# Loading rows of a fused attention and mixture-of-experts kernel by tiles, and adding the experts' rows ahead of the shared part

## The chip, the core and the metric

The kernel runs on one core of a Trainium2 chip. The metric is the time on the device from launch to end, in microseconds, as the median of several runs. The core's engines are TensorE (PE in the profile; PEld is its weight load), VectorE (DVE), ScalarE (ACT), GpSimd (POOL) and SyncE (SP), which here only issues DMAs. PEq, ACTq, POOLq and SPq in a row mean the engine's own instruction queue.

## The reference

```python
# x: 8 x 512 x 512, float32; T = 4096 tokens in all
x = x + layernorm(attention(layernorm(x, g_in), attn_bias, mask) @ Wo, g_out)   # gives "x1"
logits = (x @ wt.T + repeat(g @ wg.T)) / 2                 # 8 experts
topk_w, topk_idx = top_k(softmax(logits), 2); topk_w /= topk_w.sum()
y = sum over the 2 chosen experts e of
      topk_w * ((leaky(x @ w_gate[e]) * (x @ w_up[e])) @ w_down[e])
p = (leaky(x @ sw_gate) * (x @ sw_up)) @ sw_down           # shared part, every token
out = x + y + p
```

The attention has 16 heads of 64 with one key and one value head. An expert is 256 wide, the shared part 512.

## The kernel before

The work is done in stages, one after the other, each a block that all engines leave and enter together: projections, attention, output, route, experts, shared. Every product of importance is made three times (high half by high half, high by low, low by high), with operands split by ACT (the rounded high half) and DVE (the low half, by subtraction). The unit of work is a tile of 128 tokens; there are 32, four to a sequence ("batch", index b).

- **Output stage** (`stage_output`). Per tile t: ACT and DVE split `o_in`, the attention's result; PE multiplies it with Wo (L1251 to L1253, 24 products); DVE takes statistics (L1172) and normalizes (L1182); POOL multiplies by g and adds x (L1152, L1155), which gives x1; PE transposes x1 (L1270), ACT copies the transposed tile (L1220), PE makes the logits (L1276). SP's queue is written out by hand, in this order for a step: load o_in of tile t + 2, store x1 of t - 1, load x of t + 1, store x1T of t - 2. After tiles 0 to 15 and again after tiles 16 to 19 SP waits for the stores of the first eight tiles and issues two loads of 1 MB, x1T and x1 of batch 0 and of batch 1 (L141, L136), for the next stage.
- **Route stage** (`stage_route`). DVE finds each token's two experts and its places in the lists of the experts, in a long chain of small operations. In parallel the shared part of batches 0 and 1 is computed: ACT and DVE split x1T in four chunks of 128 columns (L1416, L1569), PE makes gate and up products (L1619 to L1621), then the down products, and ACT and POOL put the result plus x1 into `partial`. PE also counts (L1660, after `both_ready`) and finds the tokens of each tile of the experts (L1667). `leak` and `hidden` are separate buffers.
- **Expert stage** (`stage_experts`). 71 tiles of 128 gathered rows. POOL gathers the rows of a tile by an indirect DMA (L149), two buffers; PE transposes them (L1873), makes gate and up, then down products for the tile before. The weights of three experts fit. SP issues the loads of experts 1 and 2 (four DMAs of 1.5 MB) and only then reports expert 0 as ready (`make_ready`, L1764). ACT copies a finished tile and stores it in `ys_d`; at the end it waits for all these stores.
- **Shared stage** (`stage_shared`). Six steps u; step u computes the shared part of batch u + 2. `gate`/`up` products for four column blocks j (24 products each), then down products for four tiles. Meanwhile the two expert rows of each token are gathered from `ys_d` (POOL, two indirect DMAs a tile, two sets of buffers) and added by DVE, weighted (L2066, two operations a tile): for the early batches to `partial` between the gate blocks, in steps 0 and 1; for batch u + 2 to `total`, after DVE has added the PSUM result and x1 (L2096). A tile can be stored only then, and the x1 of batch b + 2 is loaded behind the four stores.

What starts the next batch's split is one semaphore for both loads:

```python
act.wait_ge(x1_loaded[k], 32 * ((u + EARLY_B) // 2 + 1))
```

Of the kernel before, what the change touches and what calls it, by code (L numbers as in the profile page):

```python
# [29 lines left out]
P = 128  # L30
# [26 lines left out]
EARLY_B = 2  # L57


def build(nc, x, fside, cond, mask, g_in, null_bias, Wq, Wkv, Wo, g_out,  # L60
# [16 lines left out]
    with ExitStack() as ctx:  # L77
# [39 lines left out]
        partial = ctx.enter_context(nc.sbuf_tensor("partial", [P, EARLY_B * TB, D], F32))  # L117
        with ExitStack() as held:
# [12 lines left out]
                          rows, xg, rows_ready, xg_loaded, partial, x_added)  # L131
        stage_shared(nc, dram, psum, ident, spare, shared, route, x1, x1_loaded, x1T, partial, out)
# [860 lines left out]
def stage_output(nc, x, cond, wo_stage, wo_loaded, g_out, wt, wg, sw_gate, sw_up, sw_down, shared, dram, psum, ident,  # L993
                 pow_half, eps, spare, logits, x1_in, x1_loaded, x1T_in):

    with ExitStack() as ctx:
# [3 lines left out]
        def sem(name):  # L1000
# [25 lines left out]
        ln_stats, ln_moments, ln_shifted, ln_rstd = (sem("ln3_stats"), sem("ln3_moments"), sem("ln3_shifted"),  # L1026
                                                     sem("ln3_rstd"))
        y_ready, y_scaled, x1_ready = sem("y_ready"), sem("y_scaled"), sem("x1_ready")
# [8 lines left out]
        EARLY = T // 4  # L1037
# [29 lines left out]
        def _(sp):  # L1067
# [7 lines left out]
            def store_x1(t, k):  # L1075
                sp.wait_ge(x1_ready, t + 1)
                sp.dma_start(dram["x1"][bass.ds(t * P, P), :], x1[k][:]).then_inc(x1_stored[k], 16)
# [21 lines left out]

            def load_shared(n, w):  # L1100
                sp.dma_start(w_stage[n % 2][:], w.rearrange("(c p) n -> p c n", p=P)).then_inc(shared_loaded[n], 16)
# [32 lines left out]
        def _(pool):  # L1134
# [9 lines left out]
            def step(t, k, m):  # L1144
                pool.wait_ge(ln_moments, t + 1)
                pool.tensor_tensor(out=rstd[:, k:k + 1], in0=moments[:, k, 1:2], in1=eps[:, 0:1], op=ALU.add
                                   ).then_inc(ln_shifted, 1)
                pool.wait_ge(ln_shifted, t + 1)
                pool.tensor_tensor(out=rstd[:, k:k + 1], in0=rstd[:, k:k + 1], in1=pow_half[:, 0:1], op=ALU.pow
                                   ).then_inc(ln_rstd, 1)  # L1150
                pool.wait_ge(y_ready, t + 1)
                pool.tensor_tensor(out=x1[k][:], in0=x1[k][:], in1=g_rows[:], op=ALU.mult).then_inc(y_scaled, 1)  # L1152
                pool.wait_ge(y_scaled, t + 1)
                pool.wait_ge(x_loaded[k], 16 * m + 16)
                pool.tensor_tensor(out=x1[k][:], in0=x1[k][:], in1=x_in[k][:], op=ALU.add).then_inc(x1_ready, 1)  # L1155
# [4 lines left out]
        def _(dve):  # L1160
# [7 lines left out]
            def step(t, k, m):  # L1168
# [9 lines left out]
                dve.wait_ge(ln_rstd, t + 1)  # L1178
# [62 lines left out]
        def _(pe):  # L1241
# [23 lines left out]
            def transpose_x1(t, k):  # L1265
                pe.wait_ge(x1_ready, t + 1)
# [32 lines left out]
def stage_route(nc, dram, psum, ident, logits, shared, route, experts, experts_loaded, x1, x1_loaded, x1T,  # L1299
# [4 lines left out]
    with ExitStack() as ctx:  # L1304
# [53 lines left out]
        hidden = [sb(f"hidden4_{i}", [P, S]) for i in range(2)]  # L1358
# [19 lines left out]
        def _(pool):  # L1378
# [23 lines left out]
            pool.wait_ge(x1_loaded[0], 32)  # L1402
# [10 lines left out]
        def _(act):  # L1413
            def split_x_high(b, c):
                act.wait_ge(x1_loaded[b], 32)
# [201 lines left out]
        def _(pe):  # L1617
# [5 lines left out]
            def gate_up(b, j):  # L1623
# [47 lines left out]
            pe.wait_ge(xT_lo_ready, DC)  # L1671
# [6 lines left out]
            pe.wait_ge(xT_lo_ready, 2 * DC)  # L1678
# [11 lines left out]
def stage_experts(nc, dram, psum, ident, spare, experts, experts_loaded, route, x1, x1_loaded, x1T, rows,  # L1690
                  xg, rows_ready, xg_loaded, partial, x_added):
# [3 lines left out]
    with ExitStack() as ctx:  # L1695
# [12 lines left out]
        y_out = [sb(f"y_out{i}", [P, D]) for i in range(2)]  # L1708
# [7 lines left out]
        ys_stored = [sem(f"ys_stored{i}") for i in range(2)]  # L1716
# [43 lines left out]
        def _(sp):  # L1760
# [406 lines left out]
```

## Time and profile before

| | |
|---|---|
| median of 3 runs | 1713.74 us (1711.5 to 1713.85) |
| the profiled execution, its own time | 1716.19 us |
| its span, first to last instruction | 1714.5 us |
| mean granted TensorE clock | 0.97 |
| PE busy | 1592.4 us, 93% |
| DVE, POOL, ACT busy | 57%, 44%, 42% |

All times inside the execution are microseconds from the start of the span. The output stage begins about 780, the route stage at 1040, the expert stage at 1123, the shared stage at 1492. A row of the timeline gives start, duration, engine, line and operation, output and inputs; the brackets at its end say how long the engine had been idle and what ended that. Consecutive equal instructions are merged in one row (x4).

### The profile page before, as it was taken

To read this page: it belongs to the slowest core of one execution; us is meant where nothing else is said; L and a number is where in the kernel's file an instruction comes from. 1 tells how busy PE (TensorE), PEld (TensorE's weight loads), DVE (VectorE), ACT (ScalarE), POOL (GpSimd) and SP (SyncE) were. 2 spreads that over 40 slices of the span, in tenths; PEclk is the share of its full clock that TensorE was granted. 3 is DMA by queue.
4 is the path that set the end of the run, shared out by engine and by line. 5 is a ranking of instruction groups with operands and counts; after the bars stand their busy time and mean duration, and the time that the engine had idled before them with its cause. 6 is when DMAs were issued, how large, how long until landed. Compare 5 with 4: busy or idle time off the path is not lost. (4 is left out here: it accounts for less than half of the span.)

```text
span 1714.5 us, 36472 instructions
## 1 busy us (share of the span) xinstructions
PE 1592.4 (93%) x10236; PEld 1336.2 (78%) x10237; DVE 973.7 (57%) x2954; ACT 712.9 (42%) x1823; POOL 747.9 (44%) x1305
## 2 busy tenths in 40 slices
PE   6899996999999999996999997989999999899997
PEld 4778876998898898895887786867777788687776
DVE  5544525877777777775654456823333334365664
ACT  2232325776777777773222222123333433311211
POOL 1000245786686686784554461432222222234222
PEclk9999998999999999998999998999999999999999
DMA  6676668787676677776556652053475533247433
GB/s 228 208 240 214 217 218 225 220 234 198 204 228 199 207 225 203 213 222 173 194 185 212 214 168 105 0 221 104 177 278 211 208 109 102 98 159 228 151 109 113
DMA packets 181195, 318.11 MB, mean 186 GB/s; under 512 B 17298, under 2 KB 64962, under 8 KB 179028
## 3 DMA queue, kind: packets, MB, share of 16 engines
q1 hardware_dynamic: 150754, 251.59, 45.9%
q0 software_dynamic: 11200, 35.73, 7.0%
q10 hardware_dynamic: 19122, 29.52, 5.0%
q8 instruction: 36, 0.59, 0.1%
q14 instruction: 83, 0.68, 0.1%
HBM read 195.38 MB, written 121.39 MB: 185 GB/s over the span
## 5 line engine op out<-in xcount | busy, mean ns | idle before, releaser
L811 DVE CUSTOM_DVE_ANT_0 scores<-psum,resident 128x514 f32<-128x514 f32 (+3 forms) x512 | 245.8, 489 | 96.3 <-issue 95.9
L885 ACT ACTIVATE probs<-scores,lowest 128x514 f32<-128x514 f32 (+3 forms) x512 | 282.9, 555 | 28.4 <-DVE lowest L811 23.3
L783 POOL TENSOR_SCALAR probs<-probs,rsums 128x512 f32<-128x512 f32 (+3 forms) x512 | 263.0, 524 | 0.0
L932 PE MATMUL psum<-keys,queries 128*128 (+4 forms) x640 | 220.7, 353 | 26.7 <-DMA queries_and_ones<-q_hi_d 17.4
L944 PE MATMUL psum<-ident,probs 128*128 128x128 f32 x1280 | 234.3, 282 | 1.6 <-POOL probs L783 1.3
L932 PE MATMUL psum<-keys_lo_and_mask,queries_and_ones 128*128 (+4 forms) x640 | 184.9, 297 | 0.0
L944 PEld LDWEIGHTS psum<-ident,probs 128*128 128x128 f32 x1280 | 151.5, 142 | 28.4 <-POOL probs L783 20.2
L964 PE MATMUL psum<-probsT,v_now 128*64 128x128 f32 x2560 | 168.3, 278 | 0.9 <-DVE probsT L826 0.9
L932 PEld LDWEIGHTS psum<-keys,queries 128*128 128x128 f32 x640 | 127.2, 199 | 33.9 <-issue 18.4
L964 PEld LDWEIGHTS psum<-probsT,v_now 128*64 128x64 f32 x2560 | 137.5, 137 | 14.5 <-issue 1.9
L894 ACT ACTIVATE probsT<-psum 128x512 f32<-128x512 f32 (+2 forms) x192 | 93.8, 489 | 115.4 <-PE psum L944 102.9
L1878 PE MATMUL psum<-expert_weights,xT_hi 128*128 x284 | 122.1, 430 | 5.6 <-SPq L1764 4.5
L932 PEld LDWEIGHTS psum<-keys_lo_and_mask,queries_and_ones 128*128 128x128 f32 x640 | 125.4, 196 | 0.0
L826 DVE COPY probsT<-psum 128x512 f32<-128x512 f32 (+1 forms) x192 | 121.6, 633 | 2.7 <-PE psum L944 2.6
L1838 DVE TENSOR_TENSOR hT_lo<-psum,hT_hi 128x256 fp32r<-128x256 f32 x71 | 30.1, 424 | 161.0 <-ACT hT_hi L1795 161.0
L1251 PE MATMUL psum<-wo_hi,oT_hi 128*128 128x512 f32 x256 | 108.7, 425 | 13.6 <-DVE oT_lo L1164 13.6
L1880 PE MATMUL psum<-expert_weights,xT_lo 128*128 x284 | 112.8, 397 | 0.0
L1879 PE MATMUL psum<-expert_weights,xT_hi 128*128 x284 | 112.4, 396 | 0.0
L146 POOL COPY slot_rows<-slot_tokens 128x1 int32 (+1 forms) x71 | 13.0, 183 | 227.9 <-PE psum L1873 226.2
L376 DVE SCALAR_TENSOR_TENSOR q_lo<-psum,q_hi 128x512 fp32r<-128x512 f32 x64 | 43.9, 687 | 113.1 <-ACT q_hi L482 113.0
L556 PE MATMUL psum<-xT_hi,wq_hi 128*128 128x512 f32 x256 | 105.3, 411 | 1.6 <-DVE xT_lo L368 1.6
L482 ACT ACTIVATE q_hi<-psum 128x512 fp32r<-128x512 f32 x64 | 38.3, 598 | 160.7 <-DMA q_lo_d<-q_lo 84.2
(242 smaller groups left out, 3705.8 us busy)
## 6 DMA issues: line engine op xcount, KB each, us to landing
ys_d<-y_out ACTq DMA_DIRECT2D x71, 256.0 KB
q_hi_d<-q_hi SPq DMA_DIRECT2D x64, 256.0 KB, 2.4
q_lo_d<-q_lo SPq DMA_DIRECT2D x64, 256.0 KB, 2.8
queries<-q_hi_d SPq DMA_DIRECT2D x64, 256.0 KB, 3.7
queries<-q_lo_d SPq DMA_DIRECT2D x64, 256.0 KB, 4.2
queries_and_ones<-q_hi_d SPq DMA_DIRECT2D x64, 256.0 KB, 4.5
oT_d<-o_out SPq DMA_DIRECT2D x64, 256.0 KB, 2.3
o_in<-oT_d SPq DMA_DIRECT2D x32, 512.0 KB, 4.8
```

What stands on the lines that cost most here:

```text
L556: pe.matmul(out, hi[:, c, :], xT_hi[k][:, c, :], start=(c == 0), stop=False)
L783: pool.tensor_scalar(out=row, in0=row, scalar1=rsums[:, n % RING:n % RING + 1], scalar2=1.0, op0=ALU.mult, op1=ALU.mult).then_inc(probs_sc ...
L811: dve.tensor_tensor_reduce(out=scores[n % 4][:, 0:CK[i]], in0=score_psum(n), in1=bias_of(resident, i, h), scale=1.0, scalar=3.0e38, op0=AL ...
L826: dve.tensor_copy(dst, src).then_inc(probsT_odd, 1)
L885: act.activation(probs[n % RING][:, 0:CK[i]], scores[n % 4][:, 0:CK[i]], ACT.Exp, bias=lowest[:, n % 4:n % 4 + 1], scale=-1.0, accum_out=s ...
L932: last = pe.matmul(whole[:, lo:hi], qs[hp % 2][:, n % 2, i * P:(i + 1) * P], ks[:, bass.ds((b % 2) * (AHEAD + S) + lo, hi - lo)], start=(p ...
L944: last = pe.transpose(probsT_bank[g % NB][:, at + j * P:at + (j + 1) * P], probs[n % RING][:, AHEAD + j * P:AHEAD + (j + 1) * P], ident[:])
L964: last = pe.matmul(o_bank[head * DH:(head + 1) * DH, cols], v_now[:, j * DH:(j + 1) * DH], probsT[half][:, at:at + P], start=(j == 0), sto ...
L1251: pe.matmul(out_bank[k], oT_hi[k][:, c, :], wo_hi[:, c, :], start=(c == 0), stop=False)
L1878: pe.matmul(out, hi, experts[:, bass.ds(at, D)], start=start, stop=False)
L1879: pe.matmul(out, hi, experts[:, bass.ds(at + EW, D)], start=False, stop=False)
L1880: return pe.matmul(out, lo, experts[:, bass.ds(at, D)], start=False, stop=stop)
```

## The change

Four places are changed.

1. Output stage: instead of two loads of 1 MB at two points, each step of tiles 12 to 27 ends with one load of 256 KB: x1T of one tile after an even step, x1 of one tile after an odd one; eight for each batch (`EARLY_LOADED` is the count that their readers wait for). The waits for the stores of tiles 0 to 7 are gone. Several semaphores of POOL and DVE are merged into one that counts both steps.
2. PE waits for each chunk of the split x in turn, in the first gate products, instead of for all four (route and shared stage). In the route stage `hidden` is put on `leak`'s place.
3. Expert stage: SP reports expert 0 first, then waits until the gathers of tiles 0 and 2 have landed, and only then loads experts 1 and 2. ACT no longer waits for its last stores; POOL waits for them at the start of the shared stage.
4. Shared stage: four sets of gather buffers instead of two. For batch u + 2 DVE first makes x1 plus the two expert rows, between the gate blocks, into a `total` of four tiles; the PSUM result is added last. The early batches' adds come after it, tile by tile. The load of the next x1 waits for the adds to x1 and goes ahead of the stores.

```diff
-        EARLY = T // 4
+        EARLY = 6
...
+            def load_x1T_tile(b, j):
+                sp.dma_start(x1T_in[b][:, bass.ds(j, 1), :, :].bitcast(F32).rearrange("p a c n -> p (a c n)"),
+                             dram["x1T"][bass.ds(j + TB * b, 1)].rearrange("a p n -> p (a n)")).then_inc(x1_loaded[b], 16)
...
-            for b in range(EARLY_B):
-                with sp.Fori((2, EARLY)[b], (EARLY, EARLY + 2)[b]) as m:
-                    for k in range(2):
-                        step(2 * m + k, k, m)
-                for i in range(2):
-                    sp.wait_ge(x1_stored[i], 16 * EARLY_B * TB // 2)
-                    sp.wait_ge(x1T_stored[i], 16 * EARLY_B * TB // 2)
-                sp.wait_ge(wo_lo_ready, len(WO_PARTS))
-                load_x1T(sp, dram, x1T_in, b, b, x1_loaded)
-                load_x1(sp, dram, x1_in, b, b, x1_loaded)
-            with sp.Fori(EARLY + 2, T // 2 - 1) as m:
+            with sp.Fori(2, EARLY) as m:
                 for k in range(2):
                     step(2 * m + k, k, m)
-            for t in range(T - 2, T):
+            sp.wait_ge(wo_lo_ready, len(WO_PARTS))
+            for b in range(EARLY_B):
+                with sp.Fori(0, TB) as j:
+                    step(2 * j + 2 * (EARLY + TB * b), 0, j + EARLY + TB * b)
+                    load_x1T_tile(b, j)
+                    step(2 * j + 2 * (EARLY + TB * b) + 1, 1, j + EARLY + TB * b)
+                    load_x1_tile(b, j)
+            for t in range(2 * (EARLY + TB * EARLY_B), T):
                 step(t, t % 2, t // 2)
...
-        hidden = [sb(f"hidden4_{i}", [P, S]) for i in range(2)]
+        hidden = leak
...
                     for c in range(DC):
+                        if j == 0 and dst is gate_bank:
+                            pe.wait_ge(xT_lo_ready, DC * b + c + 1)
...
-            pe.wait_ge(xT_lo_ready, DC)
...
+            make_ready(0)
+            sp.wait_ge(xg_loaded[0], 32)
             for e in range(1, PLACES):
                 load_expert(sp, dram, experts, e, experts_loaded)
-            make_ready(0)
             make_ready(1)
...
-            for k in range(2):
-                act.wait_ge(ys_stored[k], 16 * ((N + 1 - k) // 2))
...
+        RING = 4
-        TILES = [TB * b + t for u in range(LAST + 1) for b in ([u] if u < EARLY_B else []) + [u + EARLY_B]
+        TILES = [TB * b + t for u in range(LAST + 1) for b in [u + EARLY_B] + ([u] if u < EARLY_B else [])
                  for t in range(TB)]
...
             def step(u, k, m):
+                b = u + EARLY_B
                 if u + 2 <= LAST:
                     sp.wait_ge(xT_lo_ready, DC * u + DC)
-                    load_x1T(sp, dram, x1T, u + EARLY_B + 2, k, x1_loaded)
-                if u < EARLY_B:
-                    for t in range(TB):
-                        store(u, t, partial[:, TB * u + t, :])
-                b = u + EARLY_B
+                    load_x1T(sp, dram, x1T, b + 2, k, x1_loaded)
+                    sp.wait_ge(first_added, place(TB * b + TB - 1) + 1)
+                    load_x1(sp, dram, x1, b + 2, k, x1_loaded)
                 for t in range(TB):
-                    store(b, t, total[t % 2])
-                if u + 2 <= LAST:
-                    load_x1(sp, dram, x1, b + 2, k, x1_loaded)
+                    sp.wait_ge(total_ready, TB * u + t + 1)
+                    store(b, t, total[k][:, t, :], k)
+                    if u < EARLY_B:
+                        sp.wait_ge(picked_added, place(TB * u + t) + 1)
+                        store(u, t, partial[:, TB * u + t, :], k)
...
+            for k in range(2):
+                pool.wait_ge(ys_stored[k], 16 * ((USED_TILES + 1 - k) // 2))
             for q in TILES:
                 gather(q)
...
-                    if u < EARLY_B:
-                        add_picked(partial[:, TB * u + j, :], TB * u + j)
+                    if j == 0:
+                        dve.wait_ge(x1_loaded[k], x1_there(u))
+                        if u >= 2:
+                            dve.wait_ge(out_stored[k], 16 * STORES[u])
+                    add_experts(total[k][:, j, :], x1[k][:, j, :], TB * (u + EARLY_B) + j)
                 for t in range(TB):
...
-                    dve.tensor_tensor(out=total[n], in0=y_bank[n], in1=x1[k][:, t, :], op=ALU.add).then_inc(y_added, 1)
-                    dve.wait_ge(y_added, done)
-                    add_picked(total[n], q)
+                    dve.wait_ge(y_full, TB * u + t + 1)
+                    dve.wait_ge(picked_added, place(TB * (u + EARLY_B) + t) + 1)
+                    dve.tensor_tensor(out=total[k][:, t, :], in0=y_bank[t % 2], in1=total[k][:, t, :], op=ALU.add
+                                      ).then_inc(total_ready, 1)
+                    if u < EARLY_B:
+                        add_experts(partial[:, TB * u + t, :], partial[:, TB * u + t, :], TB * u + t)
```

`add_experts(acc, before, q)` waits for both gathers of tile q, then makes acc = weight 0 x row 0 + before and acc = weight 1 x row 1 + acc.

## Rows read from the trace of the kernel before

**Rows 1.** The page's first part: busy time of each engine.

```profile
PE 1592.4 (93%) x10236; PEld 1336.2 (78%) x10237; DVE 973.7 (57%) x2954; ACT 712.9 (42%) x1823; POOL 747.9 (44%) x1305
```

**Rows 2.** Busy per engine in a window: PEclk, DMA share, GB/s last.

```profile
1130.00:1140.00 10.00, 7.08 (x27) 5.49 (x27) 2.79 (x6) 1.76 (x4) 3.88 (x5) 0.83 1.02 429
```

**Rows 3.** Timeline, output stage, DVE: start, duration, instruction, [idle before <-releaser].

```profile
913.58 0.70 DVE L1172 BATCH_NORM_STATS2 stats<-psum 128x6 f32<-128x512 f32 x1 [1.85 <-PE psum L1253]
...
927.03 0.70 DVE L1172 BATCH_NORM_STATS2 stats<-psum 128x6 f32<-128x512 f32 x1 [5.78 <-PE psum L1253]
...
940.82 0.70 DVE L1172 BATCH_NORM_STATS2 stats<-psum 128x6 f32<-128x512 f32 x1 [1.67 <-PE psum L1253]
...
947.68 0.70 DVE L1172 BATCH_NORM_STATS2 stats<-psum 128x6 f32<-128x512 f32 x1 [1.85 <-PE psum L1253]
```

**Rows 4.** Timeline, output stage, SP's queue and ACT.

```profile
909.64 0.35 SPq L1069 DMA_DIRECT2D o_in<-oT_d  x1
...
919.30 1.15 ACT L1213 ACTIVATE oT_hi<-o_in 128x512 fp32r<-128x512 f32 x2 [10.08 <-DMA o_in<-oT_d]
...
935.12 0.34 SPq L1069 DMA_DIRECT2D o_in<-oT_d  x1
```

**Rows 5.** DMA issues, 850 to 906 us: last column us to landing.

```profile
o_in<-oT_d SPq DMA_DIRECT2D x8, 512.0 KB, 4.6
...
x1T_d<-x1T SPq DMA_DIRECT2D x8, 256.0 KB, 3.0
```

**Rows 6.** Timeline, end of the output stage and start of the route stage.

```profile
1039.57 0.42 DVE L1201 TENSOR_TENSOR logits<-psum,group_logits 128x256 f32<-128x256 f32 x1
...
1040.30 2.19 ACT L1416 ACTIVATE expert_weights<-x1T_in 128x512 fp32r<-128x512 f32 x4 [3.01 <-PEq L996]
...
1040.96 2.50 DVE L1569 TENSOR_TENSOR x1T_in<-x1T_in,expert_weights 128x512 fp32r<-128x512 f32 x4 [0.96 <-ACT expert_weights L1416]
...
1043.51 0.80 PE L1619 MATMUL psum<-expert_weights,shared_hi 128*128 128x512 f32 x1 [4.30 <-DVE x1T_in L1569]
```

**Rows 7.** Timeline, start of the expert stage: a gather, then PE's transposes of x rows.

```profile
1124.90 1.00 POOL L149 DMA_INDIRECT xg<-x_d,slot_rows  x1 [0.15 <-issue]
...
1127.53 0.60 PE L1873 MATMUL psum<-ident,xg 128*128 128x128 f32 x4
...
1134.56 0.66 PE L1873 MATMUL psum<-ident,xg 128*128 128x128 f32 x4 [2.92 <-DMA xg<-x_d,slot_rows]
...
1141.02 0.60 PE L1873 MATMUL psum<-ident,xg 128*128 128x128 f32 x4
...
1145.88 0.60 PE L1873 MATMUL psum<-ident,xg 128*128 128x128 f32 x4
```

**Rows 8.** Timeline, end of the expert stage and start of the shared stage.

```profile
1490.22 0.35 ACTq L1810 DMA_DIRECT2D ys_d<-y_out  x1
1492.72 0.63 ACT L2034 ACTIVATE xT_hi<-x1T_in 128x512 fp32r<-128x512 f32 x1 [2.53 <-PEq L1695]
...
1496.00 0.80 PE L2106 MATMUL psum<-xT_hi,shared_hi 128*128 128x512 f32 x1 [6.44 <-DVE xT_lo L2059]
```

**Rows 9.** Timeline of PE in the shared stage.

```profile
1526.31 0.50 PE L2106 MATMUL psum<-shared_hi,h_hi 128*128 128x512 f32 x1 [0.74 <-DVE total L2096]
...
1667.06 0.50 PE L2106 MATMUL psum<-shared_hi,h_hi 128*128 128x512 f32 x1
...
1700.14 0.50 PE L2106 MATMUL psum<-shared_hi,h_hi 128*128 128x512 f32 x1
```

**Rows 10.** The chain of work that ended last, in the shared stage.

```profile
1535.13 4.17 DMA picked<-ys_d,picked_rows
...
1541.33 5.87 DMA wo_x<-x_d
```

**Rows 11.** Timeline, last product and last add.

```profile
1705.48 0.39 PE L2108 MATMUL psum<-shared_hi,h_lo 128*128 128x512 f32 x1
...
1710.09 1.54 DVE L2066 SCALAR_TENSOR_TENSOR total<-picked,top_weights,total 128x512 f32<-128x512 f32 x2
```

More of the change, by code:

```diff
@@ L117, in build @@
         partial = ctx.enter_context(nc.sbuf_tensor("partial", [P, EARLY_B * TB, D], F32))
+        y_out = [ctx.enter_context(nc.sbuf_tensor(f"y_out{i}", [P, D], F32)) for i in range(2)]
+        ys_stored = [ctx.enter_context(nc.semaphore(f"ys_stored{i}")) for i in range(2)]
         with ExitStack() as held:
@@ L130, in build @@
             stage_experts(nc, dram, psum, ident, spare, experts, experts_loaded, route, x1, x1_loaded, x1T,
[L131 to L132 removed]
+                          rows, xg, rows_ready, xg_loaded, partial, x_added, y_out, ys_stored)
+        stage_shared(nc, dram, psum, ident, spare, shared, route, x1, x1_loaded, x1T, partial, out, ys_stored)
 def load_x1(eng, dram, x1, b, k, x1_loaded):
@@ L1923, in _, with stage_shared @@
             down(N - 1, 0)
-def stage_shared(nc, dram, psum, ident, spare, shared, route, x1, x1_loaded, x1T, partial, out):
+def stage_shared(nc, dram, psum, ident, spare, shared, route, x1, x1_loaded, x1T, partial, out, ys_stored):
     with ExitStack() as ctx:
@@ L1941, in stage_shared @@
         h_hi, h_lo = sb("h_hi", [P, SC, S], F32R), sb("h_lo", [P, SC, S], F32R)
-        rows = [sb(f"picked_rows{i}", [P, TOPK], I32) for i in range(2)]
+        rows = [sb(f"picked_rows{i}", [P, TOPK], I32) for i in range(RING)]
         xT_hi_ready, xT_lo_ready = sem("xT6_hi_ready"), sem("xT6_lo_ready")
@@ L1963, in batches, with x1_there @@
                 step(u, u % 2, (u + EARLY_B) // 2)
-        TILES = [TB * b + t for u in range(LAST + 1) for b in ([u] if u < EARLY_B else []) + [u + EARLY_B]
+        TILES = [TB * b + t for u in range(LAST + 1) for b in [u + EARLY_B] + ([u] if u < EARLY_B else [])
                  for t in range(TB)]
         place = TILES.index
+        STORES = [sum(TB * (2 if w < EARLY_B else 1) for w in range(u % 2, u, 2)) for u in range(LAST + 3)]
         def chunk(a, c):
             return a[:, c, :].rearrange("p (t n) -> p t n", t=TB)
-        def known(u):
-            return isinstance(u, int)
-        def first(u):
-            return known(u) and u == 0
-        def last(u):
-            return known(u) and u == LAST
+        def x1_there(u):
+            return EARLY_LOADED + 32 * (u // 2 + 1)
         block = ctx.enter_context(nc.Block())
@@ L2038, in step @@
                     act.wait_ge(up_full, SC * u + j + 1)
-                    if not (first(u) and j < 2):
+                    if not (u == 0 and j < 2):
                         act.wait_ge(h_lo_ready, SC * u + j - 1)
@@ L2043, in step @@
                     act.wait_ge(hidden_ready, SC * u + j + 1)
-                    if j == 0 and not first(u):
+                    if j == 0 and u:
                         act.wait_ge(y_full, TB * u)
                     act.activation(h_hi[:, j, :], hidden[j % 2], ACT.Copy).then_inc(h_hi_ready, 1)
-                    if not last(u):
+                    if u < LAST:
                         split_x_high(u + 1, 1 - k, range(j, j + 1))
@@ L2060, in split_x_low, with add_experts @@
                                       op=ALU.subtract).then_inc(xT_lo_ready, 1)
-            def add_picked(acc, q):
-                n = q % 2
-                dve.wait_ge(picked_loaded[n], 16 * TOPK * (place(q) // 2 + 1))
-                for j, added in enumerate((first_added, total_ready)):
-                    dve.scalar_tensor_tensor(out=acc, in0=picked[n][j],
-                                             scalar=route["weights"][:, j, q:q + 1], in1=acc,
-                                             op0=ALU.mult, op1=ALU.add).then_inc(added, 1)
-                    if j == 0:
-                        dve.wait_ge(first_added, place(q) + 1)
+            def add_experts(acc, before, q):
+                n = place(q) % RING
+                dve.wait_ge(picked_loaded[n], 16 * TOPK * (place(q) // RING + 1))
+                dve.scalar_tensor_tensor(out=acc, in0=picked[n][0], scalar=route["weights"][:, 0, q:q + 1], in1=before,
+                                         op0=ALU.mult, op1=ALU.add).then_inc(first_added, 1)
+                dve.wait_ge(first_added, place(q) + 1)
+                dve.scalar_tensor_tensor(out=acc, in0=picked[n][1], scalar=route["weights"][:, 1, q:q + 1], in1=acc,
+                                         op0=ALU.mult, op1=ALU.add).then_inc(picked_added, 1)
             def step(u, k, m):
@@ L2117, in step @@
             def step(u, k, m):
-                pe.wait_ge(xT_lo_ready, DC * u + DC)
                 for j in range(SC):
-                    if not (first(u) and j < 2):
+                    if not (u == 0 and j < 2):
                         pe.wait_ge(hidden_ready, SC * u + j - 1)
```

82 lines of the change are left out of this document (38 added, 44 removed).

## The prediction

> **What bounds the kernel.** I read the page's totals first: TensorE (PE) is busy 93% of the span [rows 1], so time can only come out of the spots where PE idles or runs at the lower clock. The change touches nothing before the output stage, so from there on I listed PE's idle gaps with what ended each. They are of four sorts: two holes inside the output stage, the first products of the three stages that follow, waits inside the last stage's batches, and the tail behind the last product. I price most of them by the start times of one repeated instruction, because that takes in the low clock behind a hole too. One such stretch is in [rows 2]: the mean granted clock of ten microseconds is 0.83, that is 3.4 us at 0.50 (1.2 of 2.4 GHz), or 1.7 us of progress lost.
>
> The sum is made against the profiled execution, whose span is 1714.5 us and whose own time is 1716.2 us. The median of the three timed runs is 1713.7 us; the savings are subtracted from that median.
>
> **Output stage: x1 loaded by tiles.** An undisturbed tile takes 6.86 us (DVE's stats at 940.82 and 947.68). The tile from 913.58 to 927.03 takes 13.45 us [rows 3], and the one that begins at 947.68 takes 13.8 us: 6.6 + 7.0 = 13.6 us too long. The cause is in SP's queue: two loads of 1 MB are issued ahead of the o_in load of 909.64, and ScalarE (ACT) waits 10.08 us for that until 919.30 [rows 4]. The change cuts the two pairs into sixteen loads of 256 KB, one in each of tiles 12 to 27.
> What it costs: SP issues one more DMA a step, some 0.5 us with its gap, ahead of the next o_in load. Its 0.26 MB take 0.6 us at the 429 GB/s that the full DMA engines move in [rows 2]. The o_in load issued at 935.12 [rows 4] lands 4.6 us later [rows 5], at 939.7, and ACT takes it when PE's products end at 940.82 (the same event as DVE's stats in [rows 3]). So 1.1 us are spare and 1.1 us are added, and behind ACT's split there is slack again, since the low halves are subtracted only after this tile's normalization. The cost is covered, barely. If the cover is gone, 0.5 us of lateness in each of 16 steps make 8 us. I take the full 13.6 us; bounds 5.6 and 13.6.
> Here the Trainium skill speaks against the change. The rows show 256 KB landing in 3.0 us and 512 KB in 4.6 us [rows 5], while SP issues such DMAs half a microsecond apart, so what is fixed in one overlaps with the next. The Trainium skill, page "DMA: Bandwidth & Descriptors", section "Bandwidth", says to batch transfers to at least 1 MiB, and its section on the anatomy of one DMA gives each a fixed cost of about 2.0 us. By that, twelve more DMAs are an estimated 24 us if nothing overlaps, and this part's gain of 13.6 us would turn into a loss of some 10 us.
>
> **Route stage: products chunk by chunk.** PE starts at 1043.51 after 4.30 us idle, when DVE has subtracted four chunks in 2.50 us from 1040.96 [rows 6], 0.62 us each. With a wait for each chunk it starts three chunks earlier, 1.9 us; three products at the low clock take longer than a chunk, so the later waits cost nothing. Late next are the counting products, which wait for DVE's top-two choice; I allow 0.4 us for it. I take 1.5 us; bounds 0.2 (the low clock lasts one such stretch of 1.7 us longer) and 1.9. `hidden` on the place of `leak` is the same instruction writing elsewhere: nothing.
>
> **Expert stage: rows gathered ahead of weights.** The transposes of x rows follow each other by 7.03 us (1127.53 to 1134.56) and 6.46 us, where a step takes 4.86 (1141.02 to 1145.88) [rows 7]: 3.8 us lost. The third tile's gather, issued from 1124.90 [rows 7], ran beside 6 MB of weights; PE wanted it 2.92 us before it came, 8.6 us after it was issued. Elsewhere a gather lands in 4.17 us [rows 10], so alone it is there by 1130, and PE asks at 1131.6. SP now waits for it, which starts the four weight DMAs about 5 us later and ends them about 1147. Expert 1's first tile comes after eight tiles of 4.86 us, so that is hidden. But the gathers of tiles 4 to 6 now meet the weights. One such takes 8.6 us and has 7.9 us from issue to use: 0.6 us of stall. In return, expert 0 is reported ready ahead of four DMA issues: 0.3 us. Saving 3.8 + 0.3 - 0.6 = 3.5 us; bounds 0.3 (the stall only moves one tile on) and 4.1.
>
> **Into the last stage.** ACT issues its last store at 1490.22 for 0.35 us, then waits for it to land; all engines cross into the next block and ACT starts at 1492.72 [rows 8]. Now only POOL waits for the landing, inside the next stage. A crossing costs 0.3 us (DVE ends at 1039.99, ACT begins at 1040.30 [rows 6]), so ACT starts at 1490.9, 1.8 us earlier. PE, which starts at 1496.00 after 6.44 us [rows 8], needs one chunk instead of four, 1.9 us. Together 3.7 us. POOL's gathers keep their time, and the first is used only after the first products, over 7 us on. PE's idle shrinks to 2.7 us; holes of 2.9 us were still followed by the low clock [rows 2, 7], so I count no gain of clock. Bounds: 2.5, and 5.4 where the clock stays up.
>
> **Within the last stage.** PE goes on after the first y add at 1526.31 in the first batch and at 1700.14 in the last; these five batches take 173.8 us, and the last of them 33.08 (from 1667.06) [rows 9]. The chain shows why: the x1 load goes out behind the batch's stores and takes 5.87 us [rows 10], and only then can ACT and DVE split the next x. Now that load waits only for the adds to x1, in the last quarter of the gate products; its use comes some 14 us later. The stores behind it in SP's queue are due after that anyway. The number of DVE operations is the same, and a ring of four gathers runs ahead of them. One thing moves onto PE's path: in every batch two adds of 0.76 us stand between the last h_lo and the first y add, as before only in the first two batches. There PE idled 0.74 us [rows 9]; starts lay 0.63 us further apart than in the last batch. So 4 x (33.08 + 0.63) + 33.1 = 167.9 us, saving 5.9 us. Bounds 4 (a late gather or split now and then) and 6.6.
>
> **Tail.** The last product starts at 1705.48, and DVE's last add ends at 1711.63 [rows 11], 2.87 us before the span's end. Now only the y add follows: 0.43 us after the product's start, 0.69 us long, then the same 2.87: 1709.5. That saves 5.0 us; bounds 4.5 and 5.0.
>
> **Sum.** 13.6 + 1.5 + 3.5 + 3.7 + 5.9 + 5.0 = 33.2 us, and 1713.7 - 33.2 = 1680.5 us. The lower bounds add up to 17.1 us (1696.6), the upper ones to 36.5 us (1677).
>
> **Rivals.**
> 1. The small loads get in the way: o_in late by 0.3 to 0.8 us in each of 16 steps. For it: 1.1 us spare against 1.1 added. Against it: the slack behind ACT. 5 to 13 us come back: 1685 to 1693. Chance 0.15.
> 2. The stall moves: the weights meet the next gathers and PE stops there as long as before, and the last stage starts with a longer low clock. 3 + 2 us come back: 1685. For it: the same bytes still move at the same time as some gather. Against it: those gathers have a whole step more of lead. Chance 0.15.
> 3. Slower than before. The only mechanism that repeats often enough is the o_in load in the output stage: at 33.2 / 16 = 2.1 us of delay a step everything is used up, and beyond that the kernel is slower. Against it: 2 MB ahead of o_in cost 6.6 us, so 0.26 MB should cost under 0.9 us, from which 1685 is nearer. Even the skill's estimate of 24 us leaves 9 us of gain. Chance 0.05, of which 0.02 that it just balances.
> 4. The moved waits end where others end already: only the holes and the tail count, 18.6 us, 1695. Chance 0.05.
>
> The forecast itself gets 0.60, with its own range of 1676 to 1685. The range of 1674 to 1691 takes in rival 2 and most of rival 1. A difference under 0.2% can't be told from none here. Faster 0.95, same 0.02, slower 0.03.
>
> **What would show it.** Output stage: stats of all tiles 6.9 us apart. Route: PE idle 2.4 us at its start. Experts: no wait for xg before the third tile, at most 0.6 us before tiles 4 to 6. Last stage: 2.7 us idle at its start, batches 33.7 us apart, the span ending 4 us behind the last product. The forecast is wrong if o_in waits appear in tiles 12 to 27, or if DVE waits for gathers between h_lo and the y adds.

## The result: 31.2 us less, 33.2 us forecast

After the change the kernel takes 1681.99 us (median of 4 runs, 1681.66 to 1683.16); four runs of the kernel before, beside it, have a median of 1713.2 us. The ratio is 0.982, 95% interval 0.9804 to 0.9835. The prediction had 1680.5 us, in a range of 1674 to 1691.

The profiled execution of after took 1681.98 us, with a span of 1680.2 us; that of before had a span of 1714.5 us. So the two traces lie 34.3 us apart, 3 us more than the medians. The first part of its page, against [rows 1], and then its fourth, the chain that ended last, by engine:

```profile
PE 1583.4 (94%) x10236; PEld 1330.0 (79%) x10237; DVE 974.8 (58%) x2954; ACT 714.1 (42%) x1823; POOL 748.5 (45%) x1305
...
PE 12%; DVE 0%; ACT 0%; issue 0%; DVEq 0%
```

The same number of PE instructions is busy for 9.0 us less, at a mean granted clock of 0.979 against 0.97; the other 25 us were idle time. The chain, which reaches back to the start of the last stage, holds no DMA any more, against [rows 10].

The 34.3 us (34.24 before rounding) are found again between nine landmarks, instructions that stand in both traces. This table is worked out from their start times:

| stretch | before | after | less | forecast |
|---|---|---|---|---|
| start to the first product of the output stage | 792.66 | 791.70 | 0.96 | none |
| to the last stats row of the output stage | 237.42 | 223.57 | 13.85 | 13.6 |
| to the first transposes of the expert stage | 93.52 | 90.88 | 2.64 | 1.5 |
| to the fifth tile's transposes | 22.28 | 19.23 | 3.05 | 3.5 |
| to the last block of expert down products | 342.02 | 341.95 | 0.07 | 0 |
| to the product after the first y add | 38.41 | 36.11 | 2.30 | 3.7 |
| five batches | 173.83 | 167.81 | 6.02 | 5.9 |
| to the end of the span | 14.31 | 8.96 | 5.35 | 5.0 |

The first line lies ahead of everything that the change touches.

**Output stage.** DVE's stats, against [rows 3]; one step takes 6.85 to 6.87 us where 13.45 us stood, and everywhere from the third step on:

```profile
905.54 0.70 DVE L1182 BATCH_NORM_STATS2 stats<-psum 128x6 f32<-128x512 f32 x1 [1.74 <-PE psum L1263]
...
912.39 0.70 DVE L1182 BATCH_NORM_STATS2 stats<-psum 128x6 f32<-128x512 f32 x1 [1.85 <-PE psum L1263]
...
919.25 0.70 DVE L1182 BATCH_NORM_STATS2 stats<-psum 128x6 f32<-128x512 f32 x1 [1.72 <-PE psum L1263]
```

The `o_in` waits that I named as a sign against me are there all the same. SP's queue of after in that stretch shows one small load ahead of `o_in`, and the timeline of ACT its end, against [rows 4]:

```profile
899.82 0.34 SPq L1106 DMA_DIRECT2D x1T_in<-x1T_d  x1
900.44 0.34 SPq L1074 DMA_DIRECT2D o_in<-oT_d  x1
```

```profile
905.77 1.15 ACT L1223 ACTIVATE oT_hi<-o_in 128x512 fp32r<-128x512 f32 x2 [4.70 <-DMA o_in<-oT_d]
907.44 0.60 ACT L1230 ACTIVATE x1T<-psum 128x512 f32<-128x512 f32 x1 [0.51 <-PE psum L1280]
```

ACT begins 0.23 us after the stats, that is after PE has let `oT_hi` go, so the load is late. The view of waits has 13 such rows, 58.8 us in all, twelve of them in or right behind tiles 12 to 27, and no stats row moves by it: the slack behind ACT's split takes it up.

**Starts of the three stages.** PE's first product of the route stage; the transposes of the first five expert tiles; the first product of the last stage, against [rows 6 to 8]:

```profile
1026.90 0.79 PE L1630 MATMUL psum<-expert_weights,shared_hi 128*128 128x512 f32 x1 [2.50 <-DVE x1T_in L1580]
...
1106.15 0.63 PE L1882 MATMUL psum<-ident,xg 128*128 128x128 f32 x4 [0.94 <-PEq L1314]
...
1110.37 1.06 PE L1882 MATMUL psum<-ident,xg 128*128 128x128 f32 x4
...
1115.17 0.60 PE L1882 MATMUL psum<-ident,xg 128*128 128x128 f32 x4
...
1120.46 0.66 PE L1882 MATMUL psum<-ident,xg 128*128 128x128 f32 x4 [0.26 <-DMA xg<-x_d,slot_rows]
...
1125.38 0.60 PE L1882 MATMUL psum<-ident,xg 128*128 128x128 f32 x4
...
1472.76 0.80 PE L2112 MATMUL psum<-xT_hi,shared_hi 128*128 128x512 f32 x1 [2.87 <-DVE xT_lo L2067]
```

PE is idle for 2.50 us instead of 4.30 and for 2.87 us instead of 6.44 (2.4 and 2.7 forecast). No tile waits long for `xg`; the fourth waits 0.26 us.

**Last stage.** PE after the y add, first and last batch, and the last product and add, against [rows 9] and [rows 11]:

```profile
1503.44 0.50 PE L2112 MATMUL psum<-shared_hi,h_hi 128*128 128x512 f32 x1 [0.74 <-DVE total L2101]
...
1671.25 0.50 PE L2112 MATMUL psum<-shared_hi,h_hi 128*128 128x512 f32 x1
...
1676.59 0.39 PE L2114 MATMUL psum<-shared_hi,h_lo 128*128 128x512 f32 x1
```

```profile
1677.02 0.69 DVE L2101 TENSOR_TENSOR total<-psum,total 128x512 f32<-128x512 f32 x1 [2.03 <-PE psum L2114]
```

From 1503.44 to 1671.25 are 167.81 us (33.69, 33.67, 33.69, 33.68, 33.08), and the add stands 0.43 us behind the start of the last product.

### The profile page after: what moved, and what is told of

Same layout as the page of the kernel before. It is cut to its first block and busy times, and to the rows that moved or that the text cites. A ratio compares the mean times of both kernels' runs of the same rounds, so it can differ in the third digit from the quotient of the medians.

```text
span 1680.2 us, 36541 instructions
## 1 busy us (share of the span) xinstructions
PE 1583.4 (94%) x10236; PEld 1330.0 (79%) x10237; DVE 974.8 (58%) x2954; ACT 714.1 (42%) x1823; POOL 748.5 (45%) x1305
```

## The experiments

The medians of one and the same kernel moved by several us from one session to the next: the kernel before had 1711.38 to 1717.43, and six executions of after in one session ran from 1675.6 to 1687.1. Much of it lies ahead of the change (the output stage's first product came between 789.0 and 797.1 in these traces). So each experiment is read between landmarks, and its median stands beside that. After is the base of all but the first; all of them compute the whole reference.

### One part alone, on the kernel before

The output stage's loads by tiles, put into the kernel before (the hunks of the diff from `EARLY = 6` to the loop over `j`, with `EARLY_LOADED` in the readers' waits).

> The kernel before with the output-stage part alone. My theory: the two holes behind the 1 MB loads go (13.6 us by the rows of before, 13.9 us between the same landmarks of the two profiles), and nothing else changes, so 1713.2 - 13.7 = 1699.5 us, with DVE's stats of all tiles from 4 to 31 at 6.86 us. The rival, that the small loads are in the way and the changed kernel only hides it: under 10 us gained and steps over 7 us among tiles 12 to 27.

Measured: 1705.57 us against 1717.43, ratio 0.9922 (0.9891 to 0.9953). No step from the fourth on is over 6.87 us and the stretch takes 224.18 us instead of 237.42: 13.2 us, although its first stats row came 0.36 us later behind the first product, so 13.6 us in the two holes. The last stage stays as before (8.10 us to its first product, batches 173.53). So this term stands by itself and, up to the scatter of the two traces, moves nothing to a later place; that the median gained 1.4 us less than this stretch is within the spread.

### The size of a burst in SP's queue

Three kernels keep the rest of after and load the same 4 MB in bursts of 2 MB (as before, with the waits for the stores of the first tiles, which SP's queue passes within 0.4 us), 0.5 MB and 1 MB ahead of an `o_in` load; after itself has 0.25 MB.

```diff
  (bursts of 0.5 MB)
                 with sp.Fori(0, TB) as j:
                     step(2 * j + 2 * (EARLY + TB * b), 0, j + EARLY + TB * b)
                     load_x1T_tile(b, j)
+                    load_x1_tile(b, j)
                     step(2 * j + 2 * (EARLY + TB * b) + 1, 1, j + EARLY + TB * b)
-                    load_x1_tile(b, j)
  (bursts of 1 MB)
+                with sp.Fori(0, TB // 2) as j:
+                    step(4 * j + 2 * (EARLY + TB * b), 0, 2 * j + EARLY + TB * b)
+                    for i in range(2):
+                        load_x1T_tile(b, 2 * j + i)
+                        load_x1_tile(b, 2 * j + i)
+                    step(4 * j + 2 * (EARLY + TB * b) + 1, 1, 2 * j + EARLY + TB * b)
+                    step(4 * j + 2 * (EARLY + TB * b) + 2, 0, 2 * j + 1 + EARLY + TB * b)
+                    step(4 * j + 2 * (EARLY + TB * b) + 3, 1, 2 * j + 1 + EARLY + TB * b)
```

> The changed kernel with the two pairs of 1 MB loads back. My theory: the holes come back as they were, 13.5 to 14 us, 1682.0 + 13.7 = 1695.7 us. If the parts depend on each other (the chunk waits or the freed queue cover the holes), the time is below 1692 us.

> The changed kernel, but the x1T and the x1 load of a tile go out together after every second step: 0.5 MB in one burst, the same bytes and the same number of DMAs. In the changed kernel o_in lands 0.1 to 0.3 us after PE's products end, and ACT can begin its split 1.8 us late before DVE or the copy of x1T is held up. A second 256 KB costs some 0.6 us of transfer and 0.5 us of issue, so o_in is 1.3 us late: still hidden, 1682 us within 1 us. If the 1.1 us that I counted as spare were all the slack, each of 8 bursts would cost 1.1 us: 1691 us. If a fixed cost for each DMA were what counts, nothing would change either, and e4 would not either.

> The same with four loads of 256 KB in one burst after every fourth step, 1 MB at once. o_in would be 0.2 + 3 x 0.6 (transfer) to 0.2 + 3 x 1.1 (issue too) = 2.0 to 3.5 us late against 1.8 us of slack: 0.2 to 1.7 us of hole in each of 4 bursts, 1 to 7 us, and up to 1.7 us each where the low clock follows: 1683 to 1695 us. If it is the size of a burst that makes the holes, this is the first that shows them; if the fixed cost of a DMA made them, it is as fast as the changed kernel.

Measured, from the steps between stats rows (6.86 us undisturbed):

| burst | DMAs | steps that are longer | lost in all | median |
|---|---|---|---|---|
| 0.25 MB (after) | 16 | none | 0 | 1681.99 |
| 0.5 MB | 16 | none | 0 | 1688.84 |
| 1 MB | 16 | 6.98, 7.11, 7.82, 7.01 | 1.5 | 1682.82 |
| 2 MB | 4 | 14.47, 13.62 | 14.4 | 1694.12 |

(The 7 us of the second row are, in the profiled execution, not these loads': there the stage began at 795.67, its second step took 10.05 us, and the stretch behind the fifth expert tile took 345.0 us instead of 341.95.) First the kernel with 2 MB, then the one with 1 MB: the `o_in` load as SP issues it, and who waits for it.

```profile
907.02 0.35 SPq L1074 DMA_DIRECT2D o_in<-oT_d  x1
...
918.03 1.15 ACT L1226 ACTIVATE oT_hi<-o_in 128x512 fp32r<-128x512 f32 x2 [11.35 <-DMA o_in<-oT_d]
```

```profile
945.49 0.34 SPq L1074 DMA_DIRECT2D o_in<-oT_d  x1
...
951.37 1.15 ACT L1226 ACTIVATE oT_hi<-o_in 128x512 fp32r<-128x512 f32 x2 [7.23 <-DMA o_in<-oT_d]
...
953.16 1.05 PE L1289 MATMUL psum<-wt_T,x1T 128*128 128x8 f32 x8 [0.71 <-ACT x1T L1233]
```

The load is used 11.0 us after it was issued behind 2 MB, and 5.9 us behind 1 MB (5.3 us in after, behind 0.25 MB). The last row shows how lateness reaches PE: the late split keeps ACT from copying the transposed x1, and the logits wait for the copy. Sixteen DMAs lose nothing, or 1.5 us; four DMAs lose 14.4 us. So it is not the number of DMAs that costs; the loss grows with the bytes that stand ahead of the load that is wanted. The 2 MB came in DMAs of 1 MB and the other bursts in DMAs of 256 KB, so the size of one DMA was not told apart from that of the burst. My reading that 1.1 us of spare time was all there is falls too: with 0.5 MB ACT began a split at 912.75, 1.1 us later than one step behind the split before it would have been due (904.79 + 6.86), and no stats row moved.

The Trainium skill, page "DMA: Bandwidth & Descriptors", section "Bandwidth", says to batch transfers to at least 1 MiB, for 75% or more of the peak. Here the kernel that does so is the slowest of the four in this stage: what bounds it is not the rate of the transfers but when the `o_in` load lands. The loss of 24 us that the prediction estimated from the same page's fixed cost of a DMA (given there for DMAs that GpSimd issues; these are SP's) isn't there: sixteen DMAs of 256 KB cost nothing.

### Expert weights ahead of the gathers

```diff
-            make_ready(0)
-
-            sp.wait_ge(xg_loaded[0], 32)
             for e in range(1, PLACES):
                 load_expert(sp, dram, experts, e, experts_loaded)
+            make_ready(0)
```

> The changed kernel with the loads of experts 1 and 2 issued first again, and expert 0 reported after them. My theory: the stall before the third tile's transposes is back (2.9 us idle) and with it the low clock; from the first transposes to those of the fifth tile 22.3 us instead of 19.2, so 3 us more: 1685 us. The rival, that the gathers of tiles 4 to 6 give the gain back: no difference over 1 us between the two, since each has one stall.

Measured: 1679.66 us (one execution). The transposes of the first to the fifth tile lie 21.40 us apart; in the eleven traces with the new order it was 18.14 to 19.23. The third and the fifth wait:

```profile
1117.00 0.66 PE L1880 MATMUL psum<-ident,xg 128*128 128x128 f32 x4 [1.56 <-DMA xg<-x_d,slot_rows]
...
1127.62 0.66 PE L1880 MATMUL psum<-ident,xg 128*128 128x128 f32 x4 [0.68 <-DMA xg<-x_d,slot_rows]
```

So the old order costs 2.2 to 3.3 us at this place. The whole execution was none the slower all the same: the way into the last stage took 3.3 us less than in after, and the stretch behind the fifth tile 1.2 us less. Both vary as much between kernels that do the same there (see the last section), so neither can be put down to the order of the loads, and the one total does not show the gain.

### Waits for the whole split, and ACT waiting for its stores

The first undoes the waits chunk by chunk in both stages, the second lets ACT wait for its last stores again.

```diff
  (whole split; the same in the shared stage, with DC * u + DC)
-                        if j == 0 and dst is gate_bank:
-                            pe.wait_ge(xT_lo_ready, DC * b + c + 1)
+            pe.wait_ge(xT_lo_ready, DC)
             for j in range(SC):
                 gate_up(0, j)
  (ACT waits)
             store_y(N - 1, 0, N // 2)
+            for k in range(2):
+                act.wait_ge(ys_stored[k], 16 * ((N + 1 - k) // 2))
```

> The changed kernel with PE waiting for all four chunks again, in the route and the shared stage. PE's idle before the first product 4.4 instead of 2.5 us in the route stage and 4.8 instead of 2.9 in the shared stage: 3.8 us more, less 0.4 us in the route stage where PE then finds the counting products ready: 1685.4 us. If DVE's chain sets the route stage's end in any case, only 1.9 us more.

> The changed kernel with ACT waiting for its last stores again at the end of the expert stage. The crossing moves from 0.45 us behind ACT's last issue to 2.1 us behind it: 1.7 us more, 1683.7 us; POOL's first gather stays where it is against the last down product. If the low clock, not the crossing, is what keeps the start of the shared stage from gaining, the time changes by under 1 us.

Measured, one execution each: 1683.57 and 1686.38 us. With the whole split, PE is idle for 4.31 us (2.50 in after) at the start of the route stage and for 4.68 us (2.87) at that of the last stage: 1.8 us at each, of the 1.9 us that I had put on each. With ACT waiting, the last stage's idle time is 4.58 us: 1.7 us, where I had 1.8.

Less than that reaches the instructions behind. From the last block of expert down products to the product after the first y add, after takes 36.11 us, the kernel with ACT's wait 37.08: 0.97 us, because more of the time at the low clock then falls on idle time. By this measure the second theory of that expectation (under 1 us) holds; the rest of the 4.4 us by which this execution was longer lies ahead of that stretch, mostly in the first steps of the output stage and in what precedes it. With the whole split the same stretch takes 36.18 us at a mean granted clock of 0.95; the kernel with bursts of 1 MB, also at 0.95, took 34.41, so 1.8 us where the clock is the same. Here is the first product of that stage, first with the whole split, then with ACT's wait:

```profile
1475.13 0.61 PE L2112 MATMUL psum<-xT_hi,shared_hi 128*128 128x512 f32 x1 [4.68 <-DVE xT_lo L2067]
```

```profile
1477.53 0.80 PE L2114 MATMUL psum<-xT_hi,shared_hi 128*128 128x512 f32 x1 [4.58 <-DVE xT_lo L2069]
```

### Two sets of gather buffers instead of four

```diff
-        RING = 4
+        RING = 2
```

> The changed kernel with two sets of gather buffers instead of four. A gather for two tiles on can then start only when DVE has added, and takes 2.7 us on POOL and 4 us to land, 6.9 us in all, against 5.5 us from one gate block to the next with two in flight: 11 us. So it should still arrive in time in steps 2 to 5; in steps 0 and 1, where the early tiles follow every 2.7 us, DVE should wait up to 1.5 us a tile, off PE's path as long as PE is in the next gate block: 1682 to 1684 us. If the ring is what made the batches shorter, the batches come to 34.5 us or more: over 1687 us.

Measured: 1692.63 us (one execution). The batches take 39.75, 38.15, 33.68, 33.68 and 33.07 us, 178.3 in all: 10.5 us more than in after, 4.5 more than in before. My expectation missed; its other case, over 1687 us, came. DVE in the first step of the last stage, then the view of waits over the whole execution (in all, times, longest):

```profile
1512.53 0.75 DVE L2073 SCALAR_TENSOR_TENSOR partial<-picked,top_weights,partial 128x512 f32<-128x512 f32 x1 [6.95 <-DMA picked<-ys_d,picked_rows]
...
1521.48 0.75 DVE L2073 SCALAR_TENSOR_TENSOR partial<-picked,top_weights,partial 128x512 f32<-128x512 f32 x1 [4.76 <-DMA picked<-ys_d,picked_rows]
```

```profile
DVE partial L2073 <- DMA picked<-ys_d,picked_rows: 22.0, 4, 6.9
```

All four long waits are for gathers of the early batches, whose adds come tile by tile behind the y adds. With two sets the gather for the next tile can only start when a set is free, DVE stops there in its order, and the next batch's `hidden` stands behind it, and PE waits for that:

```profile
1524.40 0.50 PE L2112 MATMUL psum<-xT_hi,shared_hi 128*128 128x512 f32 x1 [4.19 <-DVE hidden L2086]
```

From the third batch on, where no early batch is left, the ring makes no difference.

### x1 loaded behind the stores

```diff
+                for t in range(TB):
+                    ... (the stores, unchanged)
+                if u + 2 <= LAST:
                     sp.wait_ge(first_added, place(TB * b + TB - 1) + 1)
                     load_x1(sp, dram, x1, b + 2, k, x1_loaded)
-                for t in range(TB):
-                    ... (the stores, unchanged)
```

> The changed kernel with the next x1 load behind the batch's stores again. The last store's y add now ends right behind PE's last product of the batch, so the load goes out about 0.7 us later than that and takes 5.9 us, while ACT wants it for the next split about 7.5 us after PE's last product of the batch (one gate block, then leak and the rounded high half). My theory: just in time or up to 1.5 us late, most of it hidden since the split has a whole gate phase before its use; in steps 0 and 1, where the early tiles' stores are in between, up to 4 us late: 1682 to 1686 us. If the late x1 load alone made the long batches of the kernel before, two batches reach 35 us or more: 1687 us or more.

Measured: 1691.62 us, ratio 0.9847 (0.9822 to 0.9873). Batches 37.28, 37.35, 33.68, 33.72, 33.08: 7.3 us more than in after, and a miss again. In the first two steps eight stores stand ahead of the load (four in the later ones), and SP waits for DVE's adds to the early batches with them; the load goes out at 1515.52 and is used 11.0 us later, where I had counted 5.9 us for its landing; ACT waits for it.

```profile
1515.52 0.50 SPq L141 DMA_DIRECT2D wo_x<-x_d  x1
...
1526.52 0.63 ACT L2043 ACTIVATE xT_hi<-x1T_in 128x512 fp32r<-128x512 f32 x1 [5.55 <-DMA wo_x<-x_d]
```

So the saving within the last stage needs at least two of its pieces together, the early load and the ring of four; without either, the batches take longer than before. What the adds ahead of the PSUM result are worth alone was not tried.

### The fourth tile's add behind the first two y adds, and later weights

The 0.74 us that PE idles ahead of a y add come from the two adds of the fourth tile, as forecast. In this kernel they are made after the first two y adds:

```diff
-                    add_experts(total[k][:, j, :], x1[k][:, j, :], TB * (u + EARLY_B) + j)
+                    if j < SC - 1:
+                        add_experts(total[k][:, j, :], x1[k][:, j, :], TB * (u + EARLY_B) + j)
...
+                add_y(0)
+                add_y(1)
+                add_experts(total[k][:, TB - 1, :], x1[k][:, TB - 1, :], TB * (u + EARLY_B) + TB - 1)
+                add_early(0)
+                add_y(2)
...
```

> The changed kernel with the experts' rows of the fourth tile added after the first two y adds instead of before them. My theory: PE's idle of 0.74 us in each of five batches goes down to about 0.1 us, 0.63 us each, 3.2 us in all: 1678.8 us, the batches 33.1 us apart. If those 0.74 us are not DVE's two adds but the landing of the y bank, nothing changes: 1682 us.

> The changed kernel once more, beside e10 on the same chip, so that the two can be compared: 1682 us within 1.5 us.

Measured: 1680.65 us (5 executions, ratio 0.9808, 0.9783 to 0.9833) against 1681.79 us for after beside it (6, ratio 0.9795, 0.9771 to 0.9819): the totals can't tell them apart. The trace can. The batches are 33.04, 33.08, 33.06, 33.08 and 33.08, in sum 165.34 against 167.81 us, 2.5 us less, and PE's idle time behind each of the first five y adds is 0.10 us instead of 0.74. The first of these five lies ahead of the five batches, in a stretch that varied from 32.8 to 36.1 us with the add in its old place and takes 33.9 us here, so its 0.6 us can't be read from that stretch. PE behind the first y add:

```profile
1496.94 0.50 PE L2126 MATMUL psum<-shared_hi,h_hi 128*128 128x512 f32 x1
```

On top of it the last kernel lets SP wait for the gather of the fourth tile as well before it loads the weights of experts 1 and 2:

```diff
             sp.wait_ge(xg_loaded[0], 32)
+            sp.wait_ge(xg_loaded[1], 32)
```

> The kernel of the fourth-add run, and SP waits for the gather of the fourth tile as well before it loads experts 1 and 2 (some 4 us later). If the stall moves with the contention by one tile, as my rival 2 had it, the interval from the third to the fourth tile's transposes falls from 5.2 to 6.4 us to at most 5.0, and one of the next two intervals grows in its place; the first four intervals together take 18.6 to 19.2 us as in the changed kernel with a low clock, up to 0.7 less. If the contention ends because the later gathers are asked for early enough, all intervals are at 4.9 and the four together under 18.5 us. The expert stage's end is then held by nothing: expert 1's first tile comes 30 us later. Total within 1.5 us of the fourth-add run.

Measured: 1677.12 us (4 executions, ratio 0.9795, 0.9759 to 0.9831). First to fifth tile 19.00 us, as without it (19.08); a wait of 0.31 us now stands at 1134.7, ahead of the seventh tile. The meeting of gathers and weights only moves on. By PE's idle time behind five y adds (0.64 us each) both of these kernels are some 3 us better than after, 2.5 us of it seen between landmarks; neither is shown faster by its total.

## Why the prediction was right, and where it was off

**Output stage (13.6, measured 13.85).** The cause was as stated; putting the big loads back into after costs 14.4 us. One figure in it was wrong: I had "1.1 us are spare and 1.1 us are added". The load is 0.2 us late and more already in after, so the cover by that count was gone, and the sign that I had named for a wrong forecast (`o_in` waits in tiles 12 to 27) is there. What carried the result was the half sentence on "slack again" behind ACT, whose size I had not worked out: the forecast of the full 13.6 us had luck in it. The 13.85 are 13.6 us in the two holes and 0.2 us in the first steps of the stage.

**Route stage (1.5, measured 2.6).** The start gave 1.8 us, and 0.45 came back, close to the 0.4 that I had put on the counting products. That was luck, for the step was wrong: in neither trace is PE idle ahead of the counting products. PE started 1.8 us earlier, and more of its first products fell under the low clock. Here are the first 4 us of products before and after, the granted clock third from the end:

```profile
1043.51:1047.51 4.00, 4.00 (x12) 3.21 (x13) 3.69 (x10) 0.00 (x0) 0.00 (x0) 0.63 1.00 421
1026.90:1030.90 4.00, 4.00 (x10) 3.14 (x11) 3.83 (x9) 0.78 (x2) 0.10 (x1) 0.50 0.95 375
```

The other 1.3 us lie in the last 10 us of the stage. Before, the clock was low once more there (0.83 on the mean of 1110 to 1120), and so it was in the kernel with the output loads alone; in after and the eleven other traces with the new route stage it was not, the one with the whole split included. So the waits chunk by chunk are not the cause; `hidden` on the place of `leak`, which I had put at nothing, was not tried alone, and the cause stays open.

**Expert stage (3.5, measured 3.05).** The order of the loads is worth 2.2 to 3.3 us alone. Rival 2 holds in its small half: a stall does move to the fourth tile, 0.26 us here, 0.95 us in a second profile of after, nothing to 1.4 us in the others; "0.6 us of stall" lies between. Of the working behind it, the 7.9 us from issue to use stand in no row: before, the sixth tile's gather begins 8.17 us ahead of its use and takes 0.99 us to issue, which leaves 7.2 us and makes a stall of 1.4.

**Into the last stage (3.7, measured 2.3).** This was the worst-sized term, below its lower bound of 2.5. What failed is "I count no gain of clock", as if the clock behind the hole stayed as it was; in after it was low for longer. The two pieces measure 1.8 and 1.7 us of idle time. In the trace of after, though, 2.67 us of them are seen ahead of the first product, and 0.37 us is lost behind it. The granted clock of after, in windows:

```profile
1460.00:1466.00 6.00, 5.56 (x26) 3.92 (x24) 1.89 (x5) 1.96 (x4) 0.00 (x0) 1.00 0.12 45
1466.00:1470.00 4.00, 2.57 (x6) 1.52 (x6) 0.42 (x1) 0.45 (x2) 0.00 (x0) 0.72 0.17 66
1470.00:1478.00 8.00, 5.24 (x12) 4.14 (x13) 2.50 (x4) 2.72 (x5) 4.19 (x6) 0.50 0.37 103
1478.00:1486.00 8.00, 8.00 (x37) 6.59 (x36) 3.63 (x6) 1.75 (x3) 4.93 (x7) 1.00 0.90 318
```

It fell to 0.50 (1.2 GHz) during the last block of expert down products, before the hole that I had in mind: the block and its copy took 2.60 us (1467.33 to 1469.93) instead of 1.70. The rest is the crossing, 0.45 us from ACT's store issue to its first split where I had 0.3. In nine other traces with the same start (2.87 us idle) the step from that block to the first product was 4.5 us in four, which is 3.6 us less than before, the term in full, and 4.8 to 5.4 us in five. Up to the product after the first y add, eight traces that do the same there gained 2.3 to 5.6 us.

**Within the last stage (5.9, measured 6.0), tail (5.0, measured 5.35).** Batches of 33.68 us against 33.71 worked out, the idle 0.74 us as read from [rows 9]. What I did not see is how much the ring of four carries: I spent half a sentence on it, and without it these batches would have been slower than before. The tail's 0.35 us more are the time from the last add to the end of the span, 2.5 us where I had kept 2.87.

**The sum.** 33.3 us by these terms and 0.96 us ahead of them make the 34.2 us of the two traces; the medians give 31.2 us. That 33.3 stands so close to the forecast 33.2 is luck in part, since 1.1 us too little in the route stage and 0.35 in the tail make up for 1.4 us too much into the last stage and 0.45 in the expert stage. (The prediction's upper bounds add up to 36.6 us, not 36.5.) The missing 3 us are the profiled execution of before being 3 us over its median. Rival 1 (small loads in the way), rival 3 and rival 4 are out.

## What to carry to other kernels

On a queue that also brings what the next step needs, size a prefetch by the bytes that may stand ahead of that load, and read the slack from the engine behind the one that waits. Take out of the stretch behind the last product all that does not need it, but count how many results then have to be held at once, since that count can become the new wait. Where whole executions scatter by as much as the edit is worth, compare the start times of one repeated instruction, and read the granted clock beside them: one trace can't size a term that a low clock follows.

## What was unexpected in the hardware

The same 2.87 us of idle time at the start of the last stage was followed by different clocks. In after it was 0.50 for the eight microseconds from 1470. In the kernel with the weights first, the same stretch:

```profile
1466.00:1470.00 4.00, 2.23 (x9) 1.26 (x8) 0.51 (x2) 0.98 (x2) 0.00 (x0) 1.00 0.17 66
1470.00:1478.00 8.00, 5.13 (x23) 4.23 (x23) 2.50 (x4) 2.79 (x5) 4.07 (x6) 1.00 0.34 99
```

With the fourth add moved it was 0.50 already at 1466 to 1470 and back at 0.91 on the mean of 1470 to 1478. From the last block of down products to the product after the first y add, the same instructions took 32.8 to 36.1 us in the eight traces with this start and the add in its old place. The granted clock over that stretch (third from the end) sorts them, here after and the kernel with the weights first:

```profile
1467.33:1503.44 36.11, 32.50 (x127) 25.75 (x127) 19.53 (x30) 9.80 (x17) 15.74 (x23) 0.86 0.46 140
1468.35:1501.16 32.81, 29.20 (x127) 23.50 (x127) 19.52 (x30) 9.80 (x17) 16.55 (x23) 1.00 0.50 154
```

It was 0.86 in the three traces with 36.1 us, 0.90 in three with 34.5, 0.95 in the one with 34.4 and 1.00 in the one with 32.8. What decides how long the clock is low was not settled: the instructions ahead are the same, and only their start times differ by some microseconds.
